# Last layer of a small transformer: fp32 products from staged matrices, TensorE's tail inside both branches, value products per half

## What is computed

```
h = layernorm(x)                                  # normalisation 2
d = sigmoid(h @ W_delta.T + b_delta);  v = h @ W_value.T + b_value
state = (1 - d) * state + d * v                   # over the 37 tokens of an image
x = x + state
h = layernorm(x)                                  # normalisation 3
hp = h shifted by one token
xr = mu_r * h + (1 - mu_r) * hp;  xk = mu_k * h + (1 - mu_k) * hp
r = sigmoid(xr @ W_r.T);  k = relu(xk @ W_k.T) ** 2
out = x + r * (k @ W_v.T)
```

## Time and profile before

| | |
|---|---|
| profiled execution | 340.65 us, span 338.6 us |
| median of three runs | 340.74 us |
| TensorE, matmul | 324.1 us busy, 96% |
| TensorE, weight load | 304.6 us busy, 90% |
| VectorE | 216.9 us busy, 64% |
| ScalarE | 197.8 us busy, 58% |
| GpSimd | 144.5 us busy, 43% |
| granted TensorE clock, mean | 0.998 |

### The profile page before, as it was taken

How to read it: one execution, slowest core, us unless ns; L and a number is a source line. 1 busy time by engine, 2 the same in 40 slices (tenths; PEclk the granted TensorE clock), 3 DMA queues, 4 the chain that set the end, 5 groups by cost and what they waited for, 6 DMA issues and landing times.

```text
span 338.6 us, 7784 instructions
## 1 busy us (share of the span) xinstructions
PE 324.1 (96%) x3308; PEld 304.6 (90%) x3308; DVE 216.9 (64%) x379; ACT 197.8 (58%) x332; POOL 144.5 (43%) x101
## 2 busy tenths in 40 slices
PE   8999999999999999999999989999999999989875
PEld 8976877899998999999999989999999999968765
DVE  2667233555564587678839685766757688736884
ACT  4772333755645685457687456656566566537681
POOL 3143012385442323548374365665665874000231
PEclk9999999999999999999999999999999999999999
DMA  7937450003000521568756456464758351000002
GB/s 275 407 124 221 136 200 0 6 2 128 4 2 4 186 64 65 188 204 282 220 184 189 120 212 208 153 214 155 217 162 293 135 155 53 1 5 2 1 0 73
DMA packets 30499, 44.43 MB, mean 131 GB/s; under 512 B 1586, under 2 KB 19314, under 8 KB 30332
## 3 DMA queue, kind: packets, MB, share of 16 engines
q1 hardware_dynamic: 27868, 39.89, 35.8%
q0 software_dynamic: 960, 2.43, 2.3%
q10 hardware_dynamic: 1632, 1.57, 1.4%
HBM read 38.22 MB, written 5.49 MB: 129 GB/s over the span
## 4 chain that ended last, share of the span: by engine, by line
PE 78%; DVE 11%; ACT 6%; issue 2%; DMA 1%; POOL 1%; ACTq 0%; SPq 0%; DVEq 0%
PE ps L1498 21%; PE ps L1500 20%; PE ps L1499 20%; DVE c_region L937 3%; PE ps L1530 3%; PE ps L1630 3%; PE ps L1657 2%; DVE w_lo L937 2%; PE ps L1523 2%; PE ps L1615 1%; DMA v_region<-in_patches 1%; ACT w_hi L637 1%; DVE s_region L1275 1%; DVE xn_lo L937 1%; PE ps L1547 1%
## 5 line engine op out<-in xcount | busy, mean ns | idle before, releaser
L1498 PE MATMUL ps<-c_region,w_hi 128*128 128x256 f32 (+2 forms) x320 | 95.2, 297 | 2.8 <-DVE c_region L937 1.5
L1500 PE MATMUL ps<-c_region,w_lo 128*128 128x256 f32 (+2 forms) x320 | 92.1, 288 | 0.0
L1499 PE MATMUL ps<-c_region,w_hi 128*128 128x256 f32 (+2 forms) x320 | 92.0, 288 | 0.0
L1498 PEld LDWEIGHTS ps<-c_region,w_hi 128*128 128x128 f32 x320 | 61.1, 191 | 4.5 <-DVE c_region L937 2.7
L402 POOL TENSOR_TENSOR w_lo<-w_stage,w_hi 128x1024 fp32r<-128x1024 f32 x15 | 44.7, 2981 | 45.1 <-ACT w_hi L637 45.0
L1499 PEld LDWEIGHTS ps<-c_region,w_hi 128*128 128x128 f32 x320 | 61.1, 191 | 0.2
L1500 PEld LDWEIGHTS ps<-c_region,w_lo 128*128 128x128 f32 x320 | 61.0, 191 | 0.0
L937 DVE TENSOR_TENSOR c_region<-s_region,c_region 128x512 fp32r<-128x512 f32 (+1 forms) x44 | 47.9, 1088 | 18.1 <-ACT c_region L772 12.6
L637 ACT ACTIVATE w_hi<-w_stage 128x1024 fp32r<-128x1024 f32 (+1 forms) x42 | 49.6, 1192 | 4.4 <-DVE v_region L1330 4.4
L1498 PE MATMUL ps<-xn_hi,w_hi 128*128 128x296 f32 x152 | 47.7, 314 | 1.1 <-DVE xn_lo L937 1.1
L1499 PE MATMUL ps<-xn_lo,w_hi 128*128 128x296 f32 x152 | 45.4, 299 | 0.0
(11 more groups left out here) (185 smaller groups left out, 637.1 us busy)
## 6 DMA issues: line engine op xcount, KB each, us to landing
w_stage<-in_w_gate SPq DMA_DIRECT2D x17, 512.0 KB, 4.2
w_stage<-in_w_up SPq DMA_DIRECT2D x17, 512.0 KB, 4.2
w_stage<-in_w_down SPq DMA_DIRECT2D x8, 1024.0 KB, 5.5
expert_rows<-zeros SPq DMA_DIRECT2D x1, 1792.0 KB, 13.8
v_region<-in_patches SPq DMA_DIRECT2D x3, 576.0 KB, 5.7
v_region<-expert_rows SPq DMA_DIRECT2D x1, 1536.0 KB, 7.2
expert_out<-v_region ACTq DMA_DIRECT2D x6, 256.0 KB, 3.9
v_region<-in_w_l SPq DMA_DIRECT2D x1, 1280.0 KB, 6.8
```

What stands on the lines that cost most here:

```text
L1498: mm(o, a_h, b_h, start=start, stop=False)
L1499: mm(o, a_h, b_l, start=False, stop=False)
L1500: return mm(o, a_l, b_h, start=False, stop=stop)
```

## The change

- The products of layer 1 are fp32 matmuls straight from the staged matrices and from the unsplit activations (`full`). The splits of the five matrices, of normalisation 2's result, of the two mixtures and of the squares are gone, on ScalarE and on VectorE, with `last_part`, `l1_s` and their semaphores.
- The matrices are loaded into the staging buffer `ws` itself: four into the places of the halves g1 and u1, after the lower parts of expert 7's halves are made, the fifth behind the half of the shared down matrix. The first of these transfers stands ahead of that half's reload on SyncE's queue.
- TensorE's part of layer 1 is a function, `last_layer`, called at the end of both arms. The dummies `keep_clock(4)`, `keep_clock(7)` and `keep_clock(2, 1)` are gone, (6, 1) and (8, 1) stay.
- The gate products go by half and matrix; the first four, gates(0, 0), stand between mean(2,1) and variance(2,1). The value products go per half, values(0) ahead of the second half's projections, into banks 0 to 3 instead of 4 to 7, and no longer wait for the receptance.
- On ScalarE `relu_first(0)` stands ahead of `previous(1)`. On VectorE the clearing of `xnf` stands behind the second injection, and `relu_square(0)` right behind `normal_spread(1)`, ahead of the second half's mixtures; it also waits for the mixtures of its half, whose buffer it overwrites.

```diff
-        def last_part(i):
-            if i < 4:
-                return wh[:, L1AT[i]:L1AT[i] + KD * D], wl[:, L1AT[i]:L1AT[i] + KD * D]
-            x_h, x_l = xg(NX)
-            return x_h[:, 0:KD * D], x_l[:, 0:KD * D]
+        def last_w(i, k, m):
+            o = (L1AT[i] if i < 4 else 2 * W1 + KH // 2 * D) + k * D + m * P
+            return ws[:, o:o + P]
...
-            sp.wait_ge(s["xg_mm"], E - 1)
-            sp.dma_start(l1_s, w_l1).then_inc(s["d_l1"], 16)
+            sp.wait_ge(lo_e["g1"], NX)
+            sp.wait_ge(lo_e["u1"], NX)
+            sp.dma_start(pat(ws[:], L1AT[0], [HID, 4], [1, KD * D]),
+                         w_l1[:, 0:4 * KD * D].rearrange("p (i n) -> p i n", i=4)).then_inc(s["d_l1"], 16)
             reload("dn", NX, KH // 2)
+            sp.dma_start(ws[:, 2 * W1 + KH // 2 * D:2 * W1 + KH // 2 * D + KD * D],
+                         w_l1[:, 4 * KD * D:L1W]).then_inc(s["d_l1"], 16)
...
-            def last_high(*parts):
-                act.wait_ge(s["d_l1"], 16)
-                for i in parts:
-                    r = slice(i * KD * D, (i + 1) * KD * D)
-                    a.activation(last_part(i)[0], l1_s[:, r], ACT.Copy).then_inc(s["l1_hi"], 1)
...
             square(2, 0)
             root(2, 0)
-            high(2, 0)
             square(2, 1)
             root(2, 1)
             sigmoid_tables()
-            high(2, 1)
...
-                    act.wait_ge(s["ra_mm"], 2 * i + 1)
+                    act.wait_ge(s["ra_mm"], 4 * c + m + 1)
...
             square(3, 0)
             root(3, 0)
-            act.wait_ge(s["l1_lo"], 5)
             previous(0)
             square(3, 1)
-            mix_high(0, 1, 2)
             root(3, 1)
-            mix_high(0, 0, 4)
+            relu_first(0)
             previous(1)
-            relu_first(0)
-            mix_high(1, 1, 6)
-            relu_high(0)
-            mix_high(1, 0, 8)
             sigmoid_tables()
             receptance(0)
             relu_first(1)
-            relu_high(1)
             receptance(1)
...
             centre(2, 1)
-            low(2, 0)
             normal(2, 1)
-            low(2, 1)
...
-                    dve.wait_ge(s["ra_mm"], 2 * i + 2)
+                    dve.wait_ge(s["ra_mm"], 4 * c + 3 + m)
...
             def relu_square(c):
                 dve.wait_ge(s["k_relu"], c + 1)
+                dve.wait_ge(s["mix_ok"], 4 * c + 4)
                 v.tensor_tensor(chunk(tmp[4], c), chunk(tmp[1], c), chunk(tmp[1], c), ALU.mult).then_inc(s["k_sq"], 1)
...
             link(inject(0))
-            v.memset(pat(xnf[:], 0, [T + 1, KD * B]), 0.0)
             link(states(0))
             add_states(0)
             link(inject(1))
+            v.memset(pat(xnf[:], 0, [T + 1, KD * B]), 0.0)
             centre(3, 0)
             link(states(1))
             add_states(1)
             centre(3, 1)
             mix(0, 1)
             mix(0, 0)
-            mix_low(0, 1, 1)
             normal_spread(1)
-            mix_low(0, 0, 2)
+            relu_square(0)
             mix(1, 1)
             mix(1, 0)
-            mix_low(1, 1, 3)
-            relu_square(0)
-            relu_low(0)
-            mix_low(1, 0, 4)
             relu_square(1)
-            relu_low(1)
 
             for i, (m, c) in enumerate(MC):
                 r = slice(m * N + c * NC, m * N + (c + 1) * NC)
                 dve.wait_ge(s["r_sig"], i + 1)
                 dve.wait_ge(s["vv_mm"], i + 1)
-                w = v.tensor_tensor(tmp[2][:, r], tmp[0][:, r], bank(4 + i, NC), ALU.mult)
+                w = v.tensor_tensor(tmp[2][:, r], tmp[0][:, r], bank(i, NC), ALU.mult)
...
+            def full(o, w_i, m, x, o0, width):
+                for k in range(KD):
+                    w = mm(o, last_w(w_i, k, m), x[:, k * width + o0:k * width + o0 + NC],
+                           start=(k == 0), stop=(k == KD - 1))
+                return w
+            def gates(c, w_i):
+                pe.wait_ge(s["ln_xn"], 5 + c)
+                for m in range(KD):
+                    i = KD * c + m
+                    full(bank(i + 4 * (w_i == 0), NC), w_i, m, xnf, c * NC, NT).then_inc(s["ra_mm"], 1)
+            def project(c, w_i, x, mixed):
+                pe.wait_ge(s["mix_ok"], mixed)
+                for m in range(KD):
+                    b = KD * c + m + (4 if w_i == 2 else 0)
+                    full(bank(b, NC), w_i, m, x, c * NC, N).then_inc(s["rk_mm"], 1)
+            def values(c):
+                pe.wait_ge(s["k_sq"], c + 1)
+                for m in range(KD):
+                    full(bank(KD * c + m, NC), 4, m, tmp[4], c * NC, N).then_inc(s["vv_mm"], 1)
+            def last_layer():
+                pe.wait_ge(s["b_mul"], BACK)
+                mean(2, 1)
+                pe.wait_ge(s["d_l1"], 32)
+                gates(0, 0)
+                variance(2, 1)
+                gates(0, 1)
+                gates(1, 0)
+                gates(1, 1)
+                mean(3, 0)
+                keep_clock(6, 1)
+                variance(3, 0)
+                mean(3, 1)
+                keep_clock(8, 1)
+                variance(3, 1)
+                project(0, 3, tmp[3], 2)
+                project(0, 2, tmp[2], 4)
+                values(0)
+                project(1, 3, tmp[3], 6)
+                project(1, 2, tmp[2], 8)
+                values(1)
...
                 back_down(3)
+                last_layer()
...
-            pe.wait_ge(s["b_mul"], BACK)
-            keep_clock(4)
-            mean(2, 1)
-            keep_clock(7)
-            def last(w, k, m):
-                return [x[:, k * D + m * P:k * D + (m + 1) * P] for x in last_part(w)]
-            variance(2, 1)
-            pe.wait_ge(s["l1_lo"], 5)
-            for i, (m, c) in enumerate(MC):
-                pe.wait_ge(s["ln_lo"], 5 + c)
-                for w_i, b in ((0, 4 + i), (1, i)):
-                    for k in range(KD):
-                        x_ = slice(k * NT + c * NC, k * NT + (c + 1) * NC)
-                        w = three(bank(b, NC), *last(w_i, k, m),
-                                  xh[:, x_], xl[:, x_], k == 0, k == KD - 1)
-                    w.then_inc(s["ra_mm"], 1)
-            mean(3, 0)
-            keep_clock(6, 1)
-            variance(3, 0)
-            mean(3, 1)
-            keep_clock(8, 1)
-            variance(3, 1)
-            keep_clock(2, 1)
...
-            project(0, 3, xk_h, xk_l, 1)
-            project(0, 2, xh, xl, 2)
-            project(1, 3, xk_h, xk_l, 3)
-            project(1, 2, xh, xl, 4)
-            for i, (m, c) in enumerate(MC):
-                pe.wait_ge(s["r_sig"], i + 1)
-                pe.wait_ge(s["k_lo"], c + 1)
-                for k in range(KD):
-                    x_ = slice(k * N + c * NC, k * N + (c + 1) * NC)
-                    w = three(bank(4 + i, NC), *last(4, k, m),
-                              xk_h[:, x_], xk_l[:, x_], k == 0, k == KD - 1)
-                w.then_inc(s["vv_mm"], 1)
+                last_layer()
```

More of the change, by code:

```diff
@@ L232, in vit_tower @@
             "up_lo dn0_hi dn0_lo gu_mm silu_ok gate_mul "
-            "weighted cbe_set hid_hi hid_lo dn_mm moe_mm l1_hi l1_lo ra_mm ra_sig "
-            "mix_mul mixr_mul mix_ok mix_hi mix_lo rk_mm r_sig k_relu k_sq k_hi k_lo vv_mm gated out_ok out0_ok").split()}
+            "weighted cbe_set hid_hi hid_lo dn_mm moe_mm ra_mm ra_sig "
+            "mix_mul mixr_mul mix_ok rk_mm r_sig k_relu k_sq vv_mm gated out_ok out0_ok").split()}
         d_patch = [sem(f"d_patch{i}") for i in range(3)]
@@ L820, in _ @@
                 back_high(1)
-                last_high(3)
                 back_silu(2)
@@ L825, in _ @@
                 back_silu(3)
-                last_high(4)
                 back_high(3)
@@ L846, in _ @@
                 back()
-                last_high(*range(5))
             def sigmoid_tables():
@@ L1309, in gathered_expert @@
                             weigh(t)
-                        last_low(0)
                     else:
@@ L1345, in _ @@
                 add_merged(1, 0)
-                last_low(1)
-                last_low(2)
                 back_mul(2)
@@ L1387, in _ @@
                 back()
-                for i in range(5):
-                    last_low(i)
                 centre(2, 0)
@@ L1944, in _ @@
                 variance(2, 0)
-            pe.wait_ge(s["b_mul"], BACK)
-            keep_clock(4)
-            mean(2, 1)
-            keep_clock(7)
-            def last(w, k, m):
-                return [x[:, k * D + m * P:k * D + (m + 1) * P] for x in last_part(w)]
-            variance(2, 1)
-            pe.wait_ge(s["l1_lo"], 5)
-            for i, (m, c) in enumerate(MC):
-                pe.wait_ge(s["ln_lo"], 5 + c)
-                for w_i, b in ((0, 4 + i), (1, i)):
-                    for k in range(KD):
-                        x_ = slice(k * NT + c * NC, k * NT + (c + 1) * NC)
-                        w = three(bank(b, NC), *last(w_i, k, m),
```

(31 more changed lines are left out.)

23 lines of the change are left out of this document (removed).

## The result

The changed kernel takes 339.65 us, the median of seven runs (339.01 to 339.83), against 340.77 of before on the same chip: ratio 0.9951 (0.9933 to 0.997). The forecast was 337.1 us. It is faster, but by 1.1 us instead of 3.6. On two other chips the unchanged pair gave 0.993 (`e1_after_again`, `e8_after_third`), where before takes 344.18 and 341.53 us, a gain of 2.4 and 2.0 us.

A forecast was written before the change was run, and what follows sets the result against it. TensorE was taken to bound the kernel to 298.6 us, then a chain of waits across engines. Gains of 2.25 us up to normalisation 3 and 1.33 to the end, 3.58 in all, took 340.65 to 337.1 us; range 336.2 to 338.5.

The forecast's parts named there:

- TensorE full to 298.6, the moved loads at cost zero: From 262 to 298.6 us TensorE is always busy, so removed splits gain nothing and the moved matrix loads cost zero.
- Mean and centring: Normalisation 2, second half: mean(2,1) starts at 299.56 behind the residual add, VectorE centres from 300.86, 1.58 us gained.
- rival A: VectorE's branch exit costs the 1.59 us TensorE paid, centre(2,1) 0.94 late: 337.7 us; chance 0.17 together with B.
- B: TensorE's gap near 298.6 us comes from loading instructions and stays, mean(2,1) 0.68 late: 337.7 us; chance 0.17 with rival A.
- fp32 at 0.25 us a record: Layer 1's 40 products take two fp32 records each, 0.50 us a product, 3.6 us more TensorE work in all.
- Rival C: fp32 records with changing matrices don't run 0.25 us apart; decides from 0.30, at 0.41 gives 349.3 us; chance 0.03.
- Norm 2, gates, scans: From centre(2,1) to centre(3,0): sigmoids 2.03 us sooner, scans 2.16 sooner, 2.25 us gained up to centre(3,0).
- The slack of 0.53 us: TensorE, done with the gates, could start mean(3,0) at 309.72 but waits for the residual add until 310.25.
- From normalisation 3 to the last sum: TensorE is last everywhere from project(0,3): 48 records take 12.0 us, the last add ends at 334.56, 1.33 us gained.
- rival D: Better than the sum: output halves end sooner or waits overlap, half a microsecond, 336.5 us; chance 0.06.
- Leaving the branch: With TensorE's tail in the branch, no passage before its last product; the 1.59 us gap near 298.6 us goes.
- The 4, 7 and 2 only filled waits.: The removed dummies in TensorE's tail only filled waits; the clock was expected to stay at full, 2.4 GHz.

The follow-up runs named there:

- e1_after_again: The changed kernel again, unaltered, against the kernel before on the same chip: 341.79 us, ratio 0.993.
- e8_after_third: The changed kernel a third time, unaltered, against the kernel before on a second chip: 339.57 us, ratio 0.993.
- e2: The changed kernel with TensorE's last layer called once behind both arms, against the kernel before: 340.27 us, ratio 0.9887.
- e7: Same kernel as e2, on a second chip against the kernel before: 337.21 us, ratio 0.9872.
- e11: Same kernel as e2, on a fourth chip against the kernel before: 341.43 us, ratio 0.9914.
- e10: Kernel of e2 with the second half's output in two transfers of 148 KB, against the kernel before: 340.84 us, ratio 0.9894.
- e4: The kernel before with TensorE's old last layer written in both arms, splits and dummies kept, against the kernel before: 344.45 us, ratio 1.0001.
- e6: The changed kernel with the other arm of TensorE's last branch left out, against the kernel before: 337.80 us, ratio 0.9878.
- e9: The kernel before without the four dummies keep_clock(4) ahead of mean(2,1), against the kernel before: 341.63 us, ratio 0.9992.
- e3: The changed kernel with TensorE's branch left at variance(3,1) and the eight dummies there removed, against the kernel before: 342.50 us, ratio 0.9938.
- e12: The changed kernel, tail in both arms, with the second half's output in two transfers, against the kernel before: 341.13 us, ratio 0.9914.

## Why the prediction was wrong, point by point

- **TensorE full to 298.6, the moved loads at cost zero.** Right: from 262 to 299.5 us TensorE is busy for 37.50 of 37.50 us, and no record of the products waits for a matrix.
- **Mean and centring.** Right. The mean starts 0.98 us after the residual add's start (forecast 0.88), ended by that add, and VectorE centres 0.03 to 0.04 us behind the mean's end. VectorE then waits 0.73 us for that mean, so what leaving its branch costs is at most that and hidden, as forecast, but not measured; rival A falls. TensorE's gap at 299 us did go, so B falls, but its price was too high: with the exit left in place (e2, e7, e11, e10) the path is 0.01 to 0.06 and once 0.46 us longer, not 0.68.
- **fp32 at 0.25 us a record.** Right: 0.25 to 0.26 in rows of 48 and 24 with fresh matrices. Rival C, from 0.30 on, falls. The Trainium skill (FP8 and Floating Point Precision, TensorE Precision Notes) led to an estimate of 0.55 us a product; these rows show 0.50 to 0.51.
- **Norm 2, gates, scans.** Right within 0.1 us. From the residual add's start: the sigmoids after 7.54 us (forecast 7.49), mean(3,0) after 11.68 (11.57), centring(3,0) after 12.98 (12.88). The slack of 0.53 us was 0.34.
- **From normalisation 3 to the last sum.** Right, and no better (rival D): project(0,3) after 20.45 us (20.41), the last sum's end after 33.65 (33.63). The path shrank by 3.56 us, forecast 3.58.
- **Leaving the branch. The step that failed.** I wrote that with the tail in the branch "there is no such passage before its last product" and priced what comes behind that product at nothing, because TensorE has no work there. The trace of before showed the gap but I took it for TensorE's affair alone. The passage brings packets over the engines that carry the output; it cost 1.07, 1.57 and 1.29 us in the three traces of after, 1.64 in e4. The sum left the time from the last sum to the end at 2.7 us, without a term of its own, and that is what was mis-sized: it measured 3.78, 4.28 and 4.00 us.
- **One execution for all.** The residual add's start of one execution stood for all. In traces of before and of kernels with the same code up to 278 us it lay at 298.51, 298.55, 298.68, 298.93, 299.19, 299.55 and 299.57 on chips where before takes 340.7 to 341.6 us. That is 1 us, as much as was lost at the end, and the range of 2.3 us had no term for it. The 3.56 − 1.07 to 1.57 = 2.0 to 2.5 us that remain are what e1 (2.4) and e8 (2.0) measured; in the first comparison the traced executions differ by 1.64 us, which is 3.56 − 1.07 − 0.89 within 0.04. Part of the scatter is TensorE's clock near the start, about 1 us (e6). The clock may bear on the medians too, which differ by only 1.1 us: six of after's seven executions have a mean granted clock of 0.991 to 0.993, only the traced one 0.998, and executions of the same program at 0.991 to 0.993 took 1.1 to 2.1 us longer in e8 than those at 0.996 to 0.997. Where these six lost it is open, as they are not traced, and the clocks of before's executions in that comparison are not on record.
- **"The 4, 7 and 2 only filled waits."** Not so for the 4: e9 shows that they delayed the mean, as the rebuilt path in fact counted. Of those that stay, e3 shows what the eight are worth: 1.7 us, by the clock.

Taken apart: fp32 without splits and the new order, with the tail where it was, gives 1.1 to 1.3% (e2, e7) and 0.9% (e11); the tail in both arms takes about 0.5% back.

## What to carry to other kernels

Ask of every branch where its exit falls, not only whether an engine waits there: the jump over a long arm brings instruction packets over the engines that carry the data, and its best place is one where nothing is being transferred that the end waits for and where the engine waits anyway. A term of the sum that "doesn't change", such as the 2.7 us from the last result to the end, needs a look at what newly lies beside it. And before the size of a gain near 1 us is trusted, the same point of two executions of one kernel should be compared.

## What was not expected of the hardware

- One 16 KB packet of instructions on the engines that carry a 296 KB output transfer delays its landing from 2.3 to 3.4 us (3.4 to 3.9 in four traces), and with 148 KB from 1.8 to 3.0. At an exit over the long arm the packets come in pairs, 3.0 to 3.5 us apart.
- The stall of leaving TensorE's branch is not a constant: 1.59 and 1.33 us in two traces of before, 1.45 in e9, 1.47 in e10, at most 1.02 to 1.07 in e2, e7 and e11, whose TensorE code is that of e10. Why it is shorter there stays open.
- On the two chips where before takes 344.2 and 344.6 us, all seven traces lose 2.1 to 3.6 us against e8 within 143 to 148 us, in code that no kernel here changes; e9's loses 0.7 and those of the other two chips nothing. ScalarE of e11, and then of e8, at that point:

```profile
143.82 1.05 ACT L638 ACTIVATE w_hi<-w_stage 128x1024 fp32r<-128x1024 f32 x1
147.30 0.42 ACT L660 ACTIVATE s_region<-ps 128x296 f32<-128x296 f32 x1 [2.44 <-remote]
```

```profile
141.59 1.04 ACT L638 ACTIVATE w_hi<-w_stage 128x1024 fp32r<-128x1024 f32 x1
142.69 0.42 ACT L660 ACTIVATE s_region<-ps 128x296 f32<-128x296 f32 x1
```

The idle time of 2.44 us ahead of the expert's activation is put down to no engine. What it is was not tried. It comes in two sizes on the same chip, about 2.1 us in e1, e3 and e11 and about 3.5 us in e2, e4, e10 and e12, so it is part of the scatter of the times and drops out of a ratio only on average.
